# A fused cross-attention and feed-forward layer: the third weight piece takes the transposing DMA, and the setup is reordered

## The reference

```
h  = layernorm(x)
q  = h @ Wq.T + bq;  k = ctx @ Wk.T + bk;  v = ctx @ Wv.T + bv
x  = x + (softmax(q k.T / sqrt(32) + causal) v) @ Wo.T + bo
quant(w): per block of 16, scale = max|w| / 6; round w / scale to the grid 0 .5 1 1.5 2 3 4 6; times scale
h  = quant(layernorm(x))
x  = x + quant(silu(h @ quant(w_gate).T) * (h @ quant(w_up).T)) @ quant(w_down).T
```

## Time and profile before

| | us |
|---|---|
| median of 3 runs | 1179.34 (1178.81 to 1179.55) |
| profiled execution | 1178.53 |
| its span | 1176.7 |
| PE busy | 1158.8 (98%) |
| DVE busy | 970.3 (82%) |
| ACT busy | 483.5 (41%) |
| POOL busy | 179.3 (15%) |

### The profile page before, as it was taken

One profiled execution on the slowest core, in us unless ns is written; L12 is line 12 of the kernel. 1 busy time (PEld: TensorE's weight loads), 2 busy tenths in 40 slices (PEclk: granted clock), 3 DMA queues, 4 the chain that ended last, 5 costly groups with the idle time before them and its releaser, 6 DMA issues.

```text
span 1176.7 us, 21716 instructions
## 1 busy us (share of the span) xinstructions
PE 1158.8 (98%) x6784; PEld 1057.6 (90%) x6784; DVE 970.3 (82%) x1609; ACT 483.5 (41%) x1201; POOL 179.3 (15%) x305
## 2 busy tenths in 40 slices
PE   7899999999999999999999999999999999999998
PEld 6688888888888889999999999999999999999997
DVE  6778888888888877988888888888888888888865
ACT  3556656566566553333332332233233323333321
POOL 3433333333333310000000000000000000000000
PEclk9999999999999999999999999999999999999999
DMA  7223323323344436554445345444534454453442
GB/s 240 45 89 88 111 88 110 91 84 111 108 139 148 132 108 194 150 105 86 89 89 102 70 93 99 88 88 87 105 70 93 98 90 88 82 104 76 82 85 46
DMA packets 154955, 119.30 MB, mean 101 GB/s; under 512 B 95597, under 2 KB 122301, under 8 KB 154660
## 3 DMA queue, kind: packets, MB, share of 16 engines
q1 hardware_dynamic: 154916, 118.85, 42.7%
HBM read 74.47 MB, written 24.94 MB: 84 GB/s over the span
## 4 chain that ended last, share of the span: by engine, by line
PE 78%; SPq 7%; DMA 7%; DVE 2%; ACT 2%; issue 2%; POOL 2%; POOLq 0%; DVEq 0%; ACTq 0%
PE g_ps L175 7%; PE u_ps L175 7%; PE u_ps L176 7%; PE g_ps L176 7%; PE u_ps L177 7%; PE g_ps L177 7%; PE d_ps L1436 6%; PE d_ps L1437 6%; PE d_ps L1435 6%; SPq L504 4%; DMA ws_dram<-w_rows 4%; PE o_ps L784 3%; PE s_ps L764 3%; DMA w_wide<-ws_dram 3%; POOL w_q L586 2%
## 5 line engine op out<-in xcount | busy, mean ns | idle before, releaser
L175 PE MATMUL g_ps<-wguh,xnh 128*128 128x352 f32 x496 | 162.4, 327 | 0.5 <-issue 0.5
L175 PE MATMUL u_ps<-wguh,xnh 128*128 128x352 f32 x496 | 159.9, 322 | 0.5 <-DVE hid L1576 0.5
L176 PE MATMUL u_ps<-wgul,xnh 128*128 128x352 f32 x496 | 159.8, 322 | 0.0
L176 PE MATMUL g_ps<-wgul,xnh 128*128 128x352 f32 x496 | 159.8, 322 | 0.0
L177 PE MATMUL u_ps<-wguh,xnl 128*128 128x352 f32 x496 | 159.6, 322 | 0.0
L177 PE MATMUL g_ps<-wguh,xnl 128*128 128x352 f32 x496 | 159.5, 322 | 0.0
L898 ACT ACTIVATE probs<-s_ps,nsmax 128x77 f32<-128x77 f32 x512 | 113.7, 374 | 92.2 <-DVE nsmax L990 92.2
L1576 DVE TENSOR_TENSOR hid<-u_ps,silu 128x352 f32<-128x352 f32 x128 | 66.8, 522 | 78.1 <-PE u_ps L177 75.8
L1437 PE MATMUL d_ps<-wd,hql 128*128 128x512 f32 x330 | 128.9, 391 | 0.0
L1436 PE MATMUL d_ps<-wd,hqh 128*128 128x512 f32 x330 | 128.9, 391 | 0.0
L1435 PE MATMUL d_ps<-wd,hqh 128*128 128x512 f32 x330 | 128.4, 389 | 0.0
(11 more groups left out here) (175 smaller groups left out, 2547.1 us busy)
## 6 DMA issues: line engine op xcount, KB each, us to landing
scale_wide<-st_dram SPq DMA_DIRECT2D x248, 88.0 KB, 3.4
xin<-in_x_dram SPq DMA_DIRECT2D x32, 256.0 KB, 2.8
x_dram<-x SPq DMA_DIRECT2D x32, 256.0 KB, 2.2
xin<-x_dram SPq DMA_DIRECT2D x32, 256.0 KB, 2.7
out_dram<-y SPq DMA_DIRECT2D x32, 256.0 KB, 2.1
scale_wide<-st_dram SPq DMA_DIRECT2D x248, 32.0 KB, 1.8
w_wide<-ws_dram SPq DMA_DIRECT2D x240, 32.0 KB, 1.9
wd_dram<-wd_out SPq DMA_DIRECT2D x11, 512.0 KB, 3.0
```

The costliest lines, as they stand in the source:

```text
L175: pe.matmul(out, lh, rh, start=(i == 0), stop=False)
L176: pe.matmul(out, lh, rl, start=False, stop=False)
```

## The change

`BY_DMA` goes from 3 to 2, so piece 2 takes the DMA way. Its multiplication on POOL and its transposes on PE go; its scales are transposed on PE before the loop and copied by ACT before the loop; SP issues its transposing DMA behind the 24 placements; and all steps of the loop that ask `by_dma(n - 1)` or `by_dma(n - 2)` now also run for piece 2, in iterations 1 and 2: on SP scales out and in, on POOL `scale_turned(2)`, on ACT the wait of the shift of piece 3 for the transposing DMA of piece 2 and `piece_high(2)`, on DVE the wait of the scales of piece 3 and `piece_low(2)`. On ACT the exponentials of tile 0 move behind the high halves of piece 1 and of Wo and the shift of piece 2. On DVE the values of batch 1 move ahead of the statistics of tile 2 and the scales of piece 2, and `norm_apply(2)` moves behind the low halves of piece 1 and Wo.

```diff
-BY_DMA = 3
+BY_DMA = 2
 # sp_part, behind the placements
+            grid_transposed(BY_DMA)
             for a in range(1, T + 2):
 # pool_part
             add_bias(2)
-            rescale_piece(2)
             run(pool, iteration, 1)
 # pe_part
             def transpose_piece(n):
                 pe.wait_ge(wq_ready, n + 1)
-                pe.wait_ge(xnl_ready, (1, 2, 2)[n])
-                if n == 2:
-                    pe.wait_ge(wl_ready, 2)
+                pe.wait_ge(xnl_ready, n + 1)
 ...
             def transpose_scales(n):
                 pe.wait_ge(wquant.scale_ready, n + 1)
                 pe.wait_ge(xnl_ready, min(n, T) if isinstance(n, int) else n)
+                if isinstance(n, int) and n == BY_DMA:
+                    pe.wait_ge(wl_ready, BY_DMA)
 ...
             def transpose_xn(t):
-                if isinstance(t, int) and 1 <= t <= 2:
-                    pe.wait_ge(wl_ready, 2 * t - 1)
+                if isinstance(t, int) and t == 1:
+                    pe.wait_ge(wl_ready, 1)
 ...
             def iteration(a, n, down=None):
-                if isinstance(a, int) and a == 1:
-                    transpose_piece(2)
 ...
             weight_transposed(3)
+            transpose_scales(2)
             run(pe, iteration, 1)
 # act_part
             xn_high(1)
-            exps(0)
             piece_high(1, False)
             weight_high(3)
             wquant.shift(act, 3)
-            piece_high(2, False)
+            exps(0)
+            scale_rows(2)
             run(act, iteration, 1)
 # dve_part
             def piece_rounded(n):
                 wquant.make_magic(dve, n + 1)
                 wquant.add_magic(dve, n + 1)
-                wquant.take_magic(dve, n + 1)
+                if by_dma(n):
+                    grid_values(n)
+                else:
+                    wquant.take_magic(dve, n + 1)
 ...
             xn_low(1)
+            values(1)
             norm_stats(2)
             piece_scales(2)
-            values(1)
-            norm_apply(2)
             piece_low(1, False)
             weight_low(3)
+            norm_apply(2)
             piece_rounded(2)
-            piece_low(2, False)
             run(dve, iteration, 1)
```

## The result

The changed kernel is slower: 1190.12 us median of four runs (1188.89 to 1192.07) beside 1179.44 (1178.81 to 1182.34) of the kernel before, ratio 1.0091 with a 95% interval of 1.0076 to 1.0106, so +10.7 us. Repeated in a later series it was 1188.05 against 1178.77, 1.0081 (1.0066 to 1.0096). I had forecast slower, by 6.4 us, with a range up to 1189.0; the direction was right and the time lies above the range. The profiled execution of after is the slowest of its four (1192.07 us, span 1190.3), that of before was faster than all of its timed runs (1178.53), so the two traces show a larger difference (13.5 us) than the medians do.

What follows compares the result with a forecast made beforehand. PE was taken to bound the loop from about 50 us. The late scale trip and multiplication of piece 2 gave +6.9 us, less 0.5 for an earlier loss: +6.4, a median of 1185.7 us, range 1182.0 to 1189.0.

Steps and rivals of the forecast that it cites:

- The deciding term: Scale trip behind SP's placements: POOL's multiplication of piece 2, w_q(2), starts at 60.3, making project_out(0) and project_q(3) 6.9 us later.
- the 0.5 us that I took off for another reason: PE's lateness behind the chain in before, 25.17 us for two iterations instead of 24.6, was to disappear: -0.5 us.
- The wait of the shift of piece 3: ACT's shift waits for the transposing DMA, landing at 53.4; project_q(2) starts near 55.8 instead of 52.53, hidden by later lateness.
- The link from w_q(2) to PE: Behind POOL's piece-2 multiplication: row_scale(3), DVE's norm_apply(3), then attention's low half, 4.3 us from multiplication to project_out(0).
- my own sign: PE idle before project_out(0), released by DVE's atl; a gap under 3 us there would make the forecast wrong.
- my tie for `project_out(1)`: Second turn: project_out(1) at 76.9 by the chain of POOL's multiplications and also at 76.9 by PE.
- The chain then has to keep up: After project_q(3): turns of 12.08 us against PE's 12.30; between 0 and 1.4 us more could be lost, taken as 0.
- The reordering: Exponentials later and values earlier before the loop: scores(1) near 47.8 instead of 48.13, a gain of 0.4 us, hidden.
- A: Rival: SP is free by 43.4, so the piece costs nothing and only small gains remain: 1178.4, chance 0.07.
- A2: Rival: SP free early and the exponentials don't hold PE either: 4.5 us gained, 1174.8, chance 0.04.
- B: Rival: wide loads return soon enough, only project_q(2) is late by 3.3 us: 1182.1, chance 0.05.
- C: Rival: the chain runs behind, with turns of 13.5 us and the slow return: +10.1, 1189.4, chance 0.04.

Runs made afterwards that it cites:

- e2: Changed kernel with ACT's and DVE's old orders restored, so only piece 2 by DMA is left: +8.3 us against before, ratio 1.0073.
- e3: Changed kernel with batch 1's 12 placements taken from ahead of the loop and issued two per iteration from iteration 2: +3.5 us against before.
- e12: Changed kernel with POOL's row_scale(3) and add_bias(3) ahead of scale_turned(2), and ACT's piece_high(2) in iteration 2: +9.2 us against before.
- e10: Kernel before with ACT's order alone changed (exponentials of tile 0 behind Wo's high halves and the shift of piece 2): +1.6 us, ratio 1.0007.
- e14: Changed kernel with ACT's order of before, DVE's new order kept: +10.4 us against before, ratio 1.0087.
- e15: Changed kernel with DVE's order of before, ACT's new order kept: +8.6 us against before, ratio 1.0075.
- e6: Changed kernel with SP's scales_out issued ahead of the 256 KB piece load in every iteration: +6.3 us against before, ratio 1.0059.
- e1: Kernel before with only ACT's and DVE's setup orders changed, piece 2 not by DMA: +4.0 us, ratio 1.0037.
- e8: Piece 2 by DMA with ACT's and DVE's old orders, batch 1's placements spread over iterations, scales_out ahead of the piece load: -0.6 us against before.
- e13: Piece 2 by DMA, old orders, placements spread, scales_out first, plus POOL's row_scale(3) and add_bias(3) earlier and ACT's piece_high(2) later: -2.3 us against before.
- e5: Kernel before with 8 extra DMAs into unused DRAM in SP's queue in iteration 2, ahead of scales_out(3): +2.3 us, ratio 1.0025.
- e11: Kernel before with DVE's order alone changed (values of batch 1 first, norm_apply(2) behind the low halves): +3.0 us, ratio 1.0030.
- e9: The changed kernel timed again in the later series: +9.3 us against before, ratio 1.0081.
- e7: Kernel before with SP's scales_out issued ahead of the 256 KB piece load in every iteration: +1.1 us, ratio 1.0004.

## Why the prediction was right about the side and wrong about the size

The terms up to iteration 3 held. The term that failed is what was put at nothing behind it.

*The deciding term* was right. SP's 24 placements in one row (forecast to end at 50.2; 51.7 in the trace, with everything 1.5 us later), the transposing DMA behind them, w_q(2) at 60.3 (61.76), `project_out(0)` at 64.6 (65.62), `project_q(3)` at 71.7 (72.75). The scale trip took 2.48 us (53.78 to 56.26) where I took 2.5; the 2.0 us of the Trainium skill (DMA: Bandwidth & Descriptors, anatomy of one DMA), a fit made for DMAs issued from GpSimd, would have been too short here. From `project_q(0)` the shift at iteration 3 is 6.4 us against 6.9 forecast, so that the sum, +6.4, equals it only by the 0.5 us that I took off for another reason. e2 shows that the DMA way alone makes it, and e3 that SP's queue does.

*The wait of the shift of piece 3* was right: `project_q(2)` forecast at 55.8, seen at 56.89, and hidden by the next term as said. The transposing DMA landed 2.47 us from its start and not 3.1, though the placements stood ahead of it; that was my lower bound.

*The link from w_q(2) to PE* was named right (POOL's row_scale, DVE's norm_apply, the low half `atl`), and it ends last, but it is not where PE's idle time shows. PE waited first for ACT's copy of q, which stood behind the piece's high half (1.56 us), and then 0.26 us for `atl`. So my own sign, a gap of 3 us or more at `project_out(0)`, failed: the waits of this iteration up to there are 0.77 + 1.56 + 0.26 = 2.59 us. Removing these queue places doesn't help the median (e12). The turn of the chain behind them gives nearly the same PE time, as my tie for `project_out(1)` (76.9 both ways) had it.

*The step that failed* is the one on what follows iteration 3: "The chain then has to keep up", of which I took 0 to 1.4 us as possible, took 0, subtracted 0.5 for the loss before, and wrote that all other stages are bound by PE. The runs show three things in its place.

The 0.5 us was not won back: w_q(5) at 99.67 came a turn of 13.21 us after w_q(4), and PE's iteration 5 took 13.41 us, where before's took 12.87 (12.66 in the later series), so the shift is +6.2 to +7.1 at iteration 16. Up to here the sum still holds within 0.7 us.

Then 2.9 to 3.9 us went by iteration 31. One iteration behind the slow trip of piece 23 holds 1.8 to 1.9 of them, the others 1.0 to 2.1; in after the turn of piece 21 takes 13.48 us and those of the down pieces 22 to 30, the slow one aside, 12.3 to 12.7, against PE's 12.30, so a chain without slack can cost some tenths in each. A further 0.8 to 1.1 us went between iteration 31 and feed-forward. I had read the chain only up to 114 us and not where the pieces change kind.

How much of this belongs to the change stays open. A slow trip alone cost 1.8 us in e10, with piece 2 on the old way, and the profiled executions of e14 and e15, without one, took 1186.51 and 1184.73 us, close to the forecast, while the medians of these kernels are 1190.31 and 1188.51. e6 shows that a shorter turn removes the late loss in its trace (+4.5 at iteration 16, +4.4 at 31) and brings the runs together, but its trace has no slow trip either, so the two are not separated.

*The reordering*, taken as a gain of 0.4 us, was mis-signed: +4.0 alone (e1), 2.6 at iteration 3, by a longer wait and, in the traces of e1 and e11, a drop of the granted clock behind it. In after `scores(1)` starts at 50.09, 48.6 if the later start is taken off, where I had 47.8. It was hidden in the change, as said (e2 and after start iteration 3 within 0.1 us of each other), so it did not make the error of the sum. That it adds 1 or 2 us later, e15 (+8.6), e2 (+8.3), e14 (+10.4) and after (+9.3, +10.7) suggest by their medians; their intervals overlap.

*Rivals.* A and A2 named the right quantity, when w_q(2) starts, but their bound of 53.4 (34.0 us after `project_q(0)`) is not enough where PE itself comes earlier: e8 has w_q(2) at 32.7, and its iteration 2 still takes 13.67 us, because PE is 3.1 us ahead. e13 has it at 34.2 and keeps the gain, with the two moves. B (only the transposing wait counts) fails on its own condition: w_q(2) came at 61.76 and not by 56.7. C (the chain runs behind, +10.1) had the size of the result and a chance of 0.04. It should have had far more. But it put the loss in the first turns, which took 13.60 and 13.21 us as it says and cost PE little, and not late in attention.

## What to carry to other kernels

Moving a step from a compute engine to DMA puts it in an in-order issue queue: count from when that queue is free, and look for work in it that nobody needs yet, since that can go behind. A chain of hand-overs that turns once per iteration has some slack (here 4.8 us of lateness cost 1.4, e5), and behind it all further lateness goes to the engine that is the bound. Removing the wait that shows did not help while the chain started as late as before (e12). Read such a chain over the whole loop, above all where the pieces change kind. And when a step moves earlier, look for what it now runs beside: the shorter scale trip put POOL's last multiplication beside a step of DVE, and cost 2 us at the end of attention.

## What the runs showed of the hardware

A PE wait of 2.58 us was followed by a granted clock of 0.60 over the next 4 us in after and 0.62 in e3, and 0.58 was granted between 40 and 44 us in e11; behind the same wait the clock stayed at 1.00 in e6, e9 and e14, and behind 2.67 us in e12. Waits of 2.03 to 2.24 us were followed by 0.57 to 0.70 in e6, e7, e8 and e13, while one of 2.07 us in after (56.69) left it at 1.00. So the length of the wait alone doesn't tell whether the clock falls. Waits of 0.73, 0.69 and 1.47 us in before left it at 1.00.

From the issue of a 16 KB write to DRAM to that of the DMAs that wait for it took 2.9 us in the mean behind a 256 KB load (after), and mostly 1.4 us issued ahead of it (e6). A few such trips took 4.2 to 4.7 us.

The 24 placements, small DMAs within SBUF, held SP's queue for 0.86 us each, against 0.45 us for the repeating reads.

DVE's multiplication of 128x512 values by their scales took 0.68 us without and 1.38 to 1.60 us with POOL's multiplication beside it (e6, e7, e8, e13).
